# The beginning of an attention and soft mixture-of-experts kernel rebuilt: weights issued by ScalarE, mask and sine table first, first rope sums on VectorE, first logits ahead of the second projection

## The reference

```python
# layer 1: attention on ctx, rotary positions on two axes
q = layernorm(x) @ Wq;  k, v = split(ctx @ Wkv)        # 32 heads of 8
q, k = rope(q, pos), rope(k, pos)
w = softmax(q @ k.T / sqrt(8))                         # 64 x 64 per head and sequence
x = x + (w @ v) @ Wout + bout
# layer 2: 16 experts of 128 slots each
x_ln = layernorm(x) * gamma + beta
logits = l2norm(x_ln) * scale @ l2norm(mu)             # 2048 slots
dispatch = softmax(logits, over experts); combine = softmax(logits, over all slots)
h = gelu((x_ln.T @ dispatch) @ W1 + b1); out = combine @ (h @ W2 + b2)
x = x + out
```

## Time and profile before

| | |
|---|---|
| median of three runs | 475.66 us |
| the profiled execution | 477.61 us |
| its span | 475.7 us |
| TensorE, matmul, busy | 444.3 us (93%) |
| VectorE busy | 389.0 us (82%) |
| ScalarE busy | 286.7 us (60%) |
| GpSimd busy | 182.8 us (38%) |
| chain that ended last, by engine | PE 74%, DVE 14%, POOL 4% |

### The profile page before, as it was taken

One profiled execution on the slowest core, in us unless ns is written; L12 is line 12 of the kernel. 1 busy time (PEld: TensorE's weight loads), 2 busy tenths in 40 slices (PEclk: granted clock), 3 DMA queues, 4 the chain that ended last, 5 costly groups with the idle time before them and its releaser, 6 DMA issues.

```text
span 475.7 us, 12795 instructions
## 1 busy us (share of the span) xinstructions
PE 444.3 (93%) x4816; PEld 382.1 (80%) x4816; DVE 389.0 (82%) x857; ACT 286.7 (60%) x553; POOL 182.8 (38%) x322
## 2 busy tenths in 40 slices
PE   0679999999999999999999999999999999999996
PEld 0557787878887778878888988988988988988985
DVE  6689888898889877977977977977977877887775
ACT  3457777778888666365466466457457447447443
POOL 4479998379996332114112112112112112202100
PEclk9979999999999799999999999999999999999999
DMA  8930000000003000223213223312312312312330
GB/s 231 271 152 23 3 3 23 1 4 1 3 1 72 3 2 1 52 56 83 68 52 84 68 55 77 77 50 72 83 50 66 88 50 61 99 44 55 99 92 22
DMA packets 27815, 28.54 MB, mean 60 GB/s; under 512 B 10960, under 2 KB 19072, under 8 KB 27520
## 3 DMA queue, kind: packets, MB, share of 16 engines
q1 hardware_dynamic: 27392, 27.48, 22.1%
q10 hardware_dynamic: 384, 0.52, 0.5%
HBM read 9.11 MB, written 2.10 MB: 24 GB/s over the span
## 4 chain that ended last, share of the span: by engine, by line
PE 74%; DVE 14%; POOL 4%; SPq 3%; DMA 2%; issue 2%; ACT 1%; ACTq 0%; DVEq 0%; POOLq 0%
PE bank L1025 13%; PE bank L1027 12%; PE bank L1026 12%; PE bank L1241 10%; PE bank L1121 6%; PE bank L1263 6%; PE bank L1104 3%; PE bank L1085 3%; PE bank L1142 2%; SPq L293 2%; DVE kT L758 2%; DMA xa<-in_x 2%; DVE pT L904 2%; DVE on L777 1%; DVE pb L932 1%
## 5 line engine op out<-in xcount | busy, mean ns | idle before, releaser
L904 DVE STREAM_TRANSPOSE pT<-eb 128x512 f32<-128x512 f32 x64 | 44.5, 700 | 38.3 <-ACT eb L618 35.0
L1241 PE MATMUL bank<-w_raw,eb 128*128 128x130 f32 x512 | 60.8, 276 | 1.3 <-DVE w_raw L895 1.3
L1241 PEld LDWEIGHTS bank<-w_raw,eb 128*128 128x128 f32 x512 | 58.5, 190 | 2.7 <-DVE w_raw L895 2.3
L629 ACT ACTIVATE pb<-pb 128x768 f32<-128x768 f32 (+1 forms) x48 | 37.2, 774 | 28.2 <-DVE pb L932 28.2
L1025 PE MATMUL bank<-mun_h,xlT_l 128*128 128x512 f32 x128 | 52.1, 407 | 0.0
L932 DVE TENSOR_TENSOR pb<-bank,rh 128x384 f32<-128x384 f32 x96 | 49.3, 513 | 3.3
L624 ACT CAST xlT_h<-bank 128x256 fp32r<-128x256 f32 x16 | 5.9, 372 | 76.1 <-PE bank L1213 76.1
L618 ACT ACTIVATE eb<-bank,nshift,rn 128x512 f32<-128x512 f32 x64 | 46.2, 776 | 7.8 <-PE bank L1027 7.6
L1027 PE MATMUL bank<-mun_h,xlT_h 128*128 128x512 f32 x128 | 50.5, 395 | 0.0
L545 ACT COPY pT<-bank 128x512 f32<-128x512 f32 x64 | 37.6, 588 | 21.3 <-PE bank L1104 20.5
L1026 PE MATMUL bank<-mun_l,xlT_h 128*128 128x512 f32 x128 | 50.5, 394 | 0.0
(11 more groups left out here) (159 smaller groups left out, 1155.4 us busy)
## 6 DMA issues: line engine op xcount, KB each, us to landing
mu_raw<-pT SPq DMA_DIRECT2D x248, 64.0 KB, 2.0
mu_raw<-in_L_ffn_mu SPq DMA_DIRECT2D x1, 2048.0 KB, 10.1
out<-w_raw SPq DMA_DIRECT2D x16, 128.0 KB, 1.9
xa<-in_x SPq DMA_DIRECT2D x1, 1536.0 KB, 8.5
w_raw<-in_L_ffn_W SPq DMA_DIRECT2D x2, 512.0 KB, 10.1
w_raw<-in_L_ffn_W SPq DMA_DIRECT2D x1, 1024.0 KB, 7.3
xa<-in_x SPq DMA_DIRECT2D x1, 512.0 KB, 3.5
ctile<-in_ctx SPq DMA_DIRECT2D x1, 512.0 KB, 5.2
```

The lines of the kernel that those rows point to most:

```text
L904: v.transpose(eblk[:, :, 4 * c:4 * c + 4, :].rearrange("p m e j -> p e m j"), eb[:, 4 * c:4 * c + 4, :].rearrange("p e (m j) -> p e m j", ...
L1241: m = mm(bank[HB[i]][:, n * 2 * HC:(n + 1) * 2 * HC], eb[:, e, :], xw[:, e, :], start=True, stop=True)
```

## The change

- **Loads.** ScalarE issues Wq and Wkv on its own queue, at the start of its program. SyncE loads `ctx` of tiles 0 and 1 apart from that of 2 to 7, and the order of the rest changes. W1's two halves and W2 have semaphores of their own.
- **Constants.** GpSimd clears and fills `vw`, which VectorE did. VectorE makes the head mask before all else. ScalarE loads the sine table before the weights come.
- **Tiles 0 and 1.** VectorE, not GpSimd, normalises them, behind the low half of the weights; the first steps of the angles follow, with `xT_low(0)` in between.
- **Rope sums** of tiles 0 and 1 are made by VectorE. `q_copy(0)` is VectorE's too.
- **TensorE**: `logits(0)` stands ahead of `project_qk(1)`, and `project_v(0)` behind both. So `v_copy(0)` on ScalarE comes behind `k1_copy(0)`, with the table of the exponential behind it.
- **Statistics of tiles 4 to 15**: six at the end of step 0, six in step 1 behind the first softmax group, the moments behind the second; GpSimd's `deviations` follow its rope sums of tile 2.
- **GpSimd's side work**: W1 is split before step 1, W2 in steps 5 and 6, `xw` is cleared in step 7.

```diff
             sp.dma_start(xa[:, 0:AHEAD, :], x_d[:, 0:AHEAD, :]).then_inc(x_loaded[0], 16)
-            load_ctx(0, 0, 8)
+            load_ctx(0, 0, 2)
             sp.dma_start(posb[:], pos_d).then_inc(pos_loaded, 16)
-            sp.dma_start(wqkv_raw[:, 0:KD, :], Wq...).then_inc(wqkv_loaded, 16)
-            sp.dma_start(wqkv_raw[:, KD:KD + 2, :], Wkv...).then_inc(wqkv_loaded, 16)
+            load_ctx(1, 2, 8)
             sp.dma_start(xa[:, AHEAD:TILES, :], x_d[:, AHEAD:TILES, :]).then_inc(x_loaded[1], 16)
...
+            g.memset(vw[:].rearrange("p a b c d -> p (a b c d)"), 0.0).then_inc(vw_step, 1)
...
             def step(s, *work):
-                if s + 1 < TILES:
+                if 0 < s and s + 1 < TILES:
                     rope_sums(s + 1)
+                if s == 1:
+                    pool.wait_ge(var1_ready, 2)
+                    deviations(ln1, AHEAD, TILES, r1_step, 5, r1_ready)
+                    pool.wait_ge(r1_ready, 2)
                 if s + 3 < TILES:
                     norm_x(s + 3)
                     add_bout(s + 3)
...
-            norm_x(0)
-            norm_x(1)
-            rope_sums(0)
+            pool.wait_ge(xn_ready, 2)
             norm_x(2)
+            split_w(0)
+            split_w(1)
             pool.wait_ge(bout_loaded, 16)
             for t in range(3):
                 add_bout(t)
-            step(0, (split_w, (0,)), (split_w, (1,)))
-            pool.wait_ge(var1_ready, 2)
-            deviations(ln1, AHEAD, TILES, r1_step, 5, r1_ready)
-            pool.wait_ge(r1_ready, 2)
-            step(1, (split_w, (2,)), (split_w, (3,)), (square_mu, (0,)))
-            step(2, (square_mu, (1,)), (split_w, (4,)))
+            step(0, (split_w, (2,)), (split_w, (3,)))
+            step(1, (square_mu, (0,)))
+            step(2, (square_mu, (1,)))
...
         def _(act):
+            act.dma_start(wqkv_raw[:, 0:KD, :], Wq...).then_inc(wqkv_loaded, 16)
+            act.dma_start(wqkv_raw[:, KD:KD + 2, :], Wkv...).then_inc(wqkv_loaded, 16)
+            act.wait_ge(consts_pool, 2)
+            a.activation(warm[:], mhalf[:, 0:1], ACT.Sin).then_inc(warmed, 1)
             act.wait_ge(wqkv_loaded, 32)
             a.copy(flat(wqkv[0]), flat(wqkv_raw)).then_inc(wqkv_step, 1)
...
             xT_high(0)
-            v_copy(0)
+            act.wait_ge(ang_ready, 1)
+            a.activation(ang[:], ang[:], ACT.Sin).then_inc(sin_ready, 1)
             xT_high(1)
-            q_copy(0)
+            act.wait_ge(k1_filled, 1)
             act.wait_ge(hmask_step, 2)
             k1_copy(0)
+            v_copy(0)
+            act.wait_ge(warmed, 1)
             a.activation(warm[:], hmask[:, 0:1], ACT.Exp).then_inc(warmed, 1)
...
             def step(s, norms=None):                          # VectorE
-                if s + 1 < TILES:
+                if 0 < s and s + 1 < TILES:
                     rope_products(s + 1)
                 softmax_max(s, 0)
                 softmax_sub(s, 0)
+                if s == 0:
+                    rope_products(1)
+                    rope_sums(1)
+                if s == 1:
+                    stats1(AHEAD + 6, TILES)
                 softmax_max(s, 1)
...
                 softmax_sub(s, 1)
+                if s == 1:
+                    dve.wait_ge(st1_ready, TILES)
+                    moments(st1, ln1, AHEAD, TILES, 1.0, LN_EPS, var1_step, 7, var1_ready)
...
+                if s == 0:
+                    dve.wait_ge(x_loaded[1], 16)
+                    stats1(AHEAD, AHEAD + 6)
...
             def step(s):                                      # TensorE
                 logits(s)
+                if s == 0:
+                    project_qk(1)
+                    project_v(0)
...
             project_qk(0)
-            project_v(0)
             transpose_x(1)
             transpose_kq(0)
-            project_qk(1)
```

More of the change, by code:

```diff
@@ L345, in _ @@
             g.memset(es3[:], 0.0).then_inc(b2_cleared, 1)
+            g.memset(vw[:].rearrange("p a b c d -> p (a b c d)"), 0.0).then_inc(vw_step, 1)
+            pool.wait_ge(vw_step, 1)
+            for j in range(2):
+                g.memset(vw[64 * j:64 * j + 64].rearrange("p a b c d -> p (a b c) d")[:, :, j * VC + HD], 1.0)\
+                    .then_inc(vw_step, 1)
+            pool.wait_ge(vw_step, 3)
             pool.wait_ge(consts_pool, 4)
@@ L838, in xlT_copy, with rope_sums, q_copy @@
                     .then_inc(xlT_ready, 1)
-            dve.wait_ge(wqkv_step, 1)
-            v.tensor_tensor(flat(wqkv[1]), flat(wqkv_raw), flat(wqkv[0]).bitcast(F32), ALU.subtract)\
-                .then_inc(wqkv_ready, 1)
-            xT_low(0)
+            def rope_sums(t):
+                dve.wait_ge(ropeab_done, t * 2 + 2)
+                wait(dve, q_filled, t)
+                for e in range(2):
+                    v.tensor_tensor(qkr[:].rearrange("p a (n e) -> p (a n) e", e=2)[:, :, e],
+                                    ra[:].rearrange("p h (c e) -> p (h c) e", e=2)[:, :, e],
+                                    rb[:].rearrange("p h (c e) -> p (h c) e", e=2)[:, :, 1 - e],
+                                    ALU.add).then_inc(qk_roped, 1)
+            def q_copy(t):
+                dve.wait_ge(q_filled, t + 1)
+                v.tensor_copy(qT[:], bank[6][:, DIM:2 * DIM].rearrange("p (j n) -> p j n", j=2)).then_inc(q_ready, 1)
             dve.wait_ge(sin_ready, 1)
@@ L1065, in transpose_kq @@
                 wait(pe, x1_ready, t - 2)
-                nc.tensor.transpose(bank[5][:, 3 * P:4 * P], qkr[:, 1, P:2 * P], ident[:])
-                pe.wait_ge(v_ready, t * 4 + 4)
+                nc.tensor.transpose(bank[5][:, 3 * P:4 * P], qkr[:, 1, P:2 * P], ident[:]).then_inc(k1_filled, 1)
+                wait(pe, v_ready, t * 4 + 4 if t else 0)
                 for j in range(2):
```

93 lines of the change are left out of this document (47 added, 46 removed).

## The result

| | before | after |
|---|---|---|
| median | 475.61 us (4 runs, 475.06 to 476.0) | 481.88 us (4 runs, 480.68 to 483.23) |
| profiled execution, span | 477.61, 475.7 | 482.89, 481.1 |
| VectorE, GpSimd busy | 389.0, 182.8 | 390.9, 179.3 |

The ratio is 1.0133, 95% interval 1.0098 to 1.0169: slower by 6.3 us. The forecast was 480.3, with 476.5 to 483.2 as its range. The profiled execution of the kernel before lay 2.0 above its median and that of the changed kernel 1.0 above, so the spans differ by 5.4 and the medians by 6.3. The four runs of the changed kernel have two spans, 478.9 and 479.1 at a mean granted clock of 0.989, and 481.1 and 481.4 at 0.972.

A forecast was written before the change was run, and what follows sets the result against it. The chain of waits bounds the kernel: TensorE and VectorE hand over each step, so step 3's start sets the end. Step 0's +1.45 and +3.1 for steps 1 and 2 give +4.55 on 475.66: 480.3 us, range 476.5 to 483.2.

The forecast's parts named there:

- First logits: Start of step 0: 18.65 us without collisions, 20.95 with three collisions, against 23.44 before; bounds 18.65 and 22.85.
- x: Load of x at the start: Wq and Wkv moving beside it delay it by 1.0 us, within 0 to 1.4.
- `pow`: GpSimd's first instruction of the inverse deviations: held 1.0 us by VectorE's low half of the weights, within 0 to 1.2.
- the rope sums held by GpSimd: VectorE's rope sums ahead of the first logits: held 0.3 us by GpSimd's splits, within 0 to 1.6.
- Step 0: ScalarE's copy of values and table load put the second exponential at logits + 9.2; step ends 1.45 us later.
- Step 1: VectorE gets six statistics (2.06) and the moments (1.25), less 0.56 idle: 2.75 us longer.
- Step 2: GpSimd's late deviations and sums make TensorE wait 1.2 us, not 0.9, at tile 3's turn; +2.75 becomes +3.1.
- The clock: TensorE's half-clock stretches: a second could add up to 2 us, one vanishing save up to 1.5; taken as 0.
- Rival 2: Gaps in step 1 put TensorE at 1.2 GHz for one more stretch: +4.55 + 2, 482.2 us; chance 0.12.
- Nothing after step 3 is bound to a date: From step 3 on, a step that starts later makes the end later by as much.
- Rival 1: No collision at the start costs anything, x not delayed, `pow` not held: +2.25, 477.9 us; chance 0.2.
- Rival 3: TensorE's clock rises with the first logits and stays up: faster, -1.3, 474.4 us; chance 0.1.

The follow-up runs named there:

- quiet_pool: Changed kernel, but GpSimd's first splits of W1 wait for VectorE's rope sums of tiles 0 and 1; 482.15 us, ratio 1.0114.
- x_first: Changed kernel, but Wq and Wkv on SyncE's queue behind x and positions, VectorE doing angles, `xn`, then the weights' low half; 479.73 us, ratio 1.0062.
- table_first: Changed kernel, but ScalarE loads the exponential's table ahead of the copy of tile 0's values; 482.66 us, ratio 1.0123.
- v_early: Changed kernel, but projection and copy of tile 0's values back in their place before the change; 482.21 us, ratio 1.0118.
- stats_gap: Changed kernel, but statistics of tiles 4 to 9 ahead of the first logits' maxima, the others ending step 0, moments ahead of tile 2's products; 478.52 us, ratio 1.0045.
- best2: Changed kernel with the edits of x_first, stats_gap and v_early together, GpSimd's splits of W1 left where the change has them; 474.69 us, ratio 0.9972.
- after_warm: Changed kernel with extra turns of the identity, results unread, on TensorE where it only waits; 479.49 us, ratio 1.0067.
- best1: Changed kernel with the edits of x_first, stats_gap, quiet_pool and v_early together; 477.82 us, ratio 1.0037.

## Why the prediction was right, and where it was not

The direction and most of the size were right: +4.6 forecast, +6.3 measured, +5.4 between the profiled spans. That the sum is so near is in part luck: below, two terms, those of steps 1 and 2, are near for reasons that are not, or not all, mine.

**First logits: right in kind, one term mis-sized.** Forecast 20.95, measured 21.63. x was 1.32 late (1.0 forecast), `pow` 0.80 held (1.0), and up to the products of tile 0 the dates agree, 16.45 against 16.49. The term that failed is the rope sums held by GpSimd: 0.3 forecast, 1.25 measured (2.00, and 0.76 alone in quiet_pool). Some 0.3 of that came back, since from the turn of `qkr` to the logits it was 1.76 and not 2.05. I had put the arrival of W1 only roughly there. It came at 16.83, so the whole first pair lay beside the splits. The rest of the split that ran when the sums began, 17.81 to 18.78, is 0.97 of the 1.25; and the rest of VectorE's low half when `pow` began, 8.40 to 9.34, is 0.94, of which 0.80 was paid. The Trainium skill's rule on the shared port pair (SBUF — State Buffer, "Who interferes with whom") says that the one that issues second is held until the first ends; these rows agree with it in kind and nearly in size. Its rule that transfers of different issuers share the engines (DMA: Bandwidth & Descriptors, "Issuing engines are not separate DMA queues") agrees with x's 1.32, near the upper bound of 1.4. x_first shows all three together: 2.88 at the logits.

**Step 0: right in kind, short by 1.15.** +1.45 forecast, +2.60 measured. 0.68 is the first logits. The rest lies behind them: second exponential at logits + 9.68, not + 9.2, since the logits took 2.01 at half clock and not 1.6. That ScalarE's values and table set the date is right, but not by much: in table_first and v_early VectorE takes over at logits + 8.8, 0.9 below it. I had its second group done at logits + 7.9; the sums of tile 1, held by a split too (1.85 instead of 0.76), make the difference, and they become last once ScalarE is early.

**Step 1: the cause right, the exact size in part luck.** +2.75 forecast, +2.74 measured, and stats_gap takes 3.26 out of it. The sum was made of other pieces than mine in part, two of which nearly cancel: VectorE's added work was 3.21, its idle 0.56 went, and against these stands 0.68 of waiting for TensorE at half clock; also the `nshift` of 0.66 in the kernel before, held there, takes 0.16 now.

**Step 2: the size nearly right, the cause wrong.** I had GpSimd's late deviations hold the turn of tile 3 by 1.2, for +0.35. GpSimd was late, its sums ended at 54.96 where the forecast, step 0's term included, had 54.0; but TensorE had been thrown back as far and did not wait. The step took 10.20 instead of 9.64, +0.56. The rows show what VectorE waits for in it: 0.85 at L788 for the logits (50.67), which TensorE, at half clock up to 51.5, brings late; in the kernel before it waits for nothing there. Where the moments stand ahead of the products of tile 2 and the stretch at half clock is over by tile 3, step 2 is short too: 9.58 in stats_gap, 9.26 in best2. With the moments inside step 1 and the stretch over by tile 3 (after_warm) it takes 9.98. That is read from rows; no run tests it by itself.

**The clock: I had put 0, and that failed.** Rival 2 had a new stretch at half clock in step 1 as +2 on top. The stretch came, at 44.6 to 51.5, and step 1 still took the forecast's time, though 0.68 of it was TensorE's lateness at half clock, and, as the rows read, the 0.85 of step 2 come from it as well. (The row begins with the fall of the clock; TensorE had waited since 27.04 by then.) What it costs in there is not cleanly separated: with the statistics out, step 1 takes 10.18 with a stretch (stats_gap) and 9.66 without (best2); with them in, 13.44, and 12.46 in after_warm, where it begins at 39. Over all of the beginning after_warm puts a price on half clock in the changed kernel: 3.53 at tile 4, and a ratio of 1.0067 (1.0043 to 1.0091) instead of 1.0133 (1.0098 to 1.0169), about 3 us. In the kernel before such turns are worth 0.33% (0.14 to 0.53), some 1.6, and nothing at tile 4. So what the change costs has to be read between kernels that both have them: 2.36 at tile 4 instead of 5.89, 3.8 between the profiled spans instead of 5.4, and 1.0067 against 0.9967 in time, 1.0% or some 4.8 instead of 6.3. By the dates more than half of the loss at the beginning hangs on the clock; by the times it is a quarter, which the intervals don't tell from none. The turns also leave a stretch at half clock in each kernel (from 39 and from 38 us), so they don't give the whole price.

**Nothing after step 3 is bound to a date: right.** +5.89 at tile 4, +5.72 at tile 15. What differs later is where a stretch at half clock falls around 162 to 173 us, by up to 1.3, and the two spans of the same kernel 2.3 apart go with the clock, 0.989 and 0.972. Not every spread does: of stats_gap's ten executions one spans 474.6 at 0.996 and one 479.1 at 0.993. Which event starts these late stretches stays open.

Rival 1 (no collision) fell with x, `pow` and the sums. Rival 3 (the clock stays up from the first logits) did not happen: the record is at half from 20.5 to 27 us and from 30.7 to 37.2. In best1 logits and second projection ran at full pitch (1.12 for the 32 matmuls that took 2.01), but that kernel ran at half clock from 26.4 us on.
